# First attention of a two-layer transformer kernel on one Trainium2 core: the root polynomial's middle step on GpSimd, twelve root tiles and four log tiles, and a wide PSUM ring

## The chip, the cores and the metric

One core of one Trainium2 chip runs the whole program. The metric is the device time of one execution in microseconds (us). TensorE (PE), VectorE (DVE), ScalarE (ACT), GpSimd (POOL) and SyncE (SP) run their own instruction streams and meet only in semaphores.

## The reference, cut to what matters

Two layers, each attention plus a feed-forward part, over 2048 positions of width 128. The change lies in the attention of layer 0, which has 16 heads of width 8:

```python
q, k = _l2norm(to_heads(q)), _l2norm(to_heads(k))
cos = einsum('bhsd,bhtd->bhst', q, k)
g_dist = arccos(clip(cos, -1 + EPS, 1 - EPS))
attn_score = (1 + g_dist) ** -3.2
n_r, n_c = attn_score.sum(-1), attn_score.sum(-2)
k_tilde = n_r[..., :, None] ** -1 * attn_score * n_c[..., None, :] ** -1
probs = k_tilde / maximum(k_tilde.sum(-1), 1e-12)
out = einsum('bhst,bhtd->bhsd', probs, v)
```

So each head needs a 2048 x 2048 map of arccos, then of the power -3.2 (as Exp of -3.2 times Ln of 1 + angle), column sums, and a product with the values. The rest of the program (the projections, the feed-forward parts, the second attention) is as it was.

## The kernel before, in words

`stage_attention0` works head by head. The map of a head is 16 tiles of 128 keys x 2048 queries in float32, `wt[:, k, :]`. TensorE makes the raw material in PSUM. `square(h, g)` gives half a tile (two matmuls of 512 columns, L639) of the squared sine into one of the two 1024-wide slots of `m_ps`; `ring(h, r)` gives a chunk of 512 columns (L656, L660) into one of the two 512-wide slots of `r_ps`. A matmul of the ring waits until the chunk two before it has been read (`ring_read`).

There are two ways to the angle. A **root tile** (`NQ` = 8 of them) takes a Sqrt on ScalarE out of `m_ps` (L560, two halves), and then a polynomial on VectorE in `root_tile`: four chunks of L444 (U: the root against a ring chunk), four of L450 (V: into the single buffer `two`, shown by the profile as `base`), two of L456 (1024 wide, V plus a constant times U, all in SBUF; its semaphore is `cubic`), four of L463 (F: the last factor against a ring chunk). A **log tile** (`NL` = 8) takes Ln (L568), Sigmoid (L603) and Arctan (L607) on ScalarE with four chunks of L474 on VectorE between the last two. Afterwards all tiles get Ln with a bias (`theta`, L578, by the groups in `GROUPS`) and Exp with the column sum (`score`, L587). VectorE's `values` (L484, L486) turns the column sums into weighted values, and TensorE's `weigh(h, p)` (L671, four column groups) adds a tile into `o_ps`.

Order in a head. ScalarE: table load, roots 0 to 7, table load, logs, table load, sigmoids and arctans in pairs, table load, then `theta` and `score` in turn. VectorE: `values` of the last two tiles of the head before, root tiles 0 to 2 (`RA` = 3; `finish` copies `o_ps` to `o_sb`, L492, ahead of tile 2), `finish_rows`, the eight log tiles, root tiles 3 to 7 with `values` of the first tiles among them, `stack` (four pieces of L433, the next head's operand `mst`), `values`. TensorE: two `weigh` of the head before, then squares with ring chunks strewn among them by the list `ring_to`, worked out beforehand from a pace of 0.954 us a root, 0.625 us a chunk and 2.35 us for L456, then the rest of the ring with `turn_factors` (transposes for the next head, L629) and three `weigh` inside it, six `weigh`, `start` of the next head (squares 0 and 1, ring chunks 0 and 1), and five `weigh`. GpSimd has only `monomials` (L287 to L308) once a head, and waits for `turn_factors` of that head. SyncE loads `qst` and `kst` of the next head once the ring of a head has been issued. On every engine heads 1 to 14 are a hardware loop (`Fori`; ScalarE has all 16 in it), heads 0 and 15 are written out.

Of the kernel before, what the change touches and what calls it, by code (L numbers as in the profile page):

```python
# [6 lines left out]
ALU = mybir.AluOpType  # L7
# [8 lines left out]
S = 2048  # L16
D = 128
NT = S // P
# [13 lines left out]
NL = 8  # L32
# [27 lines left out]
def stage_project0(nc, io, sb):  # L60
# [3 lines left out]
    with ExitStack() as ctx:  # L64
# [49 lines left out]
        with nc.Block() as block:  # L114
# [91 lines left out]
            @block.gpsimd  # L206
            def _(eng):
                fac = sb["fac"]
                for i, f in enumerate(F_ROWS):
                    eng.memset(fac[:, 0, :, 3 * NMON + i:3 * NMON + i + 1], GQK * GQK)  # L210
                    eng.memset(fac[:, 1, :, 3 * NMON + i:3 * NMON + i + 1], -f * GQK * GQK)
                eng.wait_ge(qkn_ready, 1)
                monomials(eng, sb, 0, mono, mono_ready)
# [69 lines left out]
def monomials(eng, sb, h, mono, mono_ready):  # L283

    qkn, xs, pr, fac = sb["qkn"], sb["mono_x"], sb["mono_p"], sb["fac"]
    steps = 3 * h
    eng.tensor_copy(xs[:, :, :, :].rearrange("p x n d -> p n x d"),  # L287
                    qkn[:, :, :].rearrange("p n (x d) -> p n x d", x=2)[:, :, :, bass.ds(h * HD0, HD0)])\
       .then_inc(mono, 1)
    eng.wait_ge(mono, steps + 1)  # L290
# [7 lines left out]
    eng.wait_ge(mono, steps + 2)  # L298
# [7 lines left out]
    eng.wait_ge(mono, steps + 3)  # L306
# [5 lines left out]
def stage_attention0(nc, io, sb):  # L312
# [7 lines left out]
    RA = 3  # L320
    GROUPS = (0, 4, NL, NL + 5, NT - 2, NT - 1, NT)
    PAIRS = tuple(range(0, NL, 2)) + (NL,)
    NM0 = 2 * NT
    NRING = 12 * NQ + 4 * NL
    NCU = 2 * NQ
    NSG = len(PAIRS) - 1

    def q_at(j):
        return 12 * j if j < RA else 12 * j + 4 * NL

    def s_at(j):
        return 12 * RA + 4 * j

# [6 lines left out]
    ROOT_US, CHUNK_US, CUBE_US, LOAD_US, LAG_US = 0.954, 0.625, 2.35, 1.3, 1.2  # L340

    def ring_time(r):

        q, z = (r, 0) if r < s_at(0) else (s_at(0), r - s_at(0)) if r < s_at(NL) else (r - 4 * NL, 4 * NL)
        return (q + z) * CHUNK_US + (q // 12 + (q % 12 >= 8)) * CUBE_US
# [4 lines left out]
    ring_to = [2 + sum(1 for r in range(2, NRING) if ring_time(r - 1) + LAG_US <= root_time(g)) for g in range(NM0)]  # L350
    with ExitStack() as ctx:
# [20 lines left out]
        st_ps = m_ps[:, :, :].rearrange("p a b -> p (a b)").bitcast(F16)  # L372

# [5 lines left out]
        cubic, sig_done = sem("cubic"), sem("sig_done")  # L379
# [5 lines left out]
        def cols(k, n=P):  # L385
            return slice(k * n, (k + 1) * n)

        with nc.Block() as block:
# [24 lines left out]
            def _(eng):  # L413
                with eng.Fori(1, H) as h:

                    eng.wait_ge(fac_turned, 4 * h)
                    eng.wait_ge(mono_ready, 1)
                    monomials(eng, sb, h, mono, mono_ready)

            @block.vector  # L420
            def _(eng):
# [5 lines left out]
                def stack(h, j):  # L427

                    eng.wait_ge(fac_turned, 4 * h + j + 1)
                    if j == 0 and not (isinstance(h, int) and h == 0):  # L430
                        eng.wait_ge(ring_ps, NRING * h)
                    half = mst[:, j % 2, cols(j // 2, S // 2)]
                    eng.tensor_scalar(half, st_ps[0:KM, cols(j, S // 2)], -1.0 if j % 2 else 1.0, None, ALU.mult)\  # L433
                       .then_inc(mst_ready, 1)

                def root_tile(h, j):

                    at = q_at(j)
                    for i in range(NCH):
                        if i % 2 == 0:  # L440
                            eng.wait_ge(m0_read, NM0 * h + 2 * j + i // 2 + 1)
                        eng.wait_ge(ring_ps, NRING * h + at + i + 1)
                        u = wt[:, j, cols(i, BANK)]
                        eng.scalar_tensor_tensor(out=u, in0=u, scalar=-B1 * S_MIN * G4, in1=r_ps[:, (at + i) % 2, :],  # L444
                                                 op0=ALU.max, op1=ALU.subtract).then_inc(ring_read, 1)
                    for i in range(NCH):

                        eng.wait_ge(ring_read, NRING * h + at + i + 1)
                        eng.wait_ge(ring_ps, NRING * h + at + NCH + i + 1)
                        eng.scalar_tensor_tensor(out=two[:, cols(i, BANK)], in0=wt[:, j, cols(i, BANK)],  # L450
                                                 scalar=-K1 * G4, in1=r_ps[:, (at + i) % 2, :],
                                                 op0=ALU.add, op1=ALU.mult).then_inc(ring_read, 1)
# [5 lines left out]
                    for i in range(NCH):  # L458
                        if i % 2 == 0:
                            eng.wait_ge(cubic, NCU * h + 2 * j + i // 2 + 1)  # L460
                        eng.wait_ge(ring_ps, NRING * h + at + 2 * NCH + i + 1)
                        u = wt[:, j, cols(i, BANK)]
                        eng.scalar_tensor_tensor(out=u, in0=u, scalar=K3 * G4 * G4 * G4, in1=r_ps[:, (at + i) % 2, :],  # L463
                                                 op0=ALU.add, op1=ALU.mult).then_inc(ring_read, 1)

                def log_tile(h, j):

                    if j in PAIRS:
                        eng.wait_ge(sig_done, NSG * h + j // 2 + 1)
                    for i in range(NCH):  # L470
# [1098 lines left out]
```

## Time and profile before

| what | value |
|---|---|
| median of 3 runs | 3972.32 us (3971.55 to 3972.55) |
| the profiled execution | 3976.55 us, its span 3974.8 us |
| PE, DVE, ACT, POOL busy in the span | 3205.7, 2999.1, 3186.7, 1201.9 us |
| mean granted TensorE clock | 0.784 |
| last Exp of one head to the last Exp of the next | 133.1 us |
| part of the span that is the first attention's heads | about 118 to 2250 us |

The span is cut into busy time of each engine, and each idle stretch is put down to what released it. Times in a timeline count from the span's start. Instructions of one engine overlap a little in the records: the distance between starts is what an instruction takes of its engine, and it is below the recorded duration.

### The profile page before, as it was taken

To read this page: it belongs to the slowest core of one execution; us is meant where nothing else is said; L and a number is where in the kernel's file an instruction comes from. 1 tells how busy PE (TensorE), PEld (TensorE's weight loads), DVE (VectorE), ACT (ScalarE), POOL (GpSimd) and SP (SyncE) were. 2 spreads that over 40 slices of the span, in tenths; PEclk is the share of its full clock that TensorE was granted. 3 is DMA by queue.
4 is the path that set the end of the run, shared out by engine and by line. 5 is a ranking of instruction groups with operands and counts; after the bars stand their busy time and mean duration, and the time that the engine had idled before them with its cause. 6 is when DMAs were issued, how large, how long until landed. Compare 5 with 4: busy or idle time off the path is not lost. (4 is left out here: it accounts for less than half of the span.)

```text
span 3974.8 us, 59836 instructions
## 1 busy us (share of the span) xinstructions
PE 3205.7 (81%) x18880; PEld 1330.2 (33%) x18880; DVE 2999.1 (75%) x4716; ACT 3186.7 (80%) x2690; POOL 1201.9 (30%) x746
## 2 busy tenths in 40 slices
PE   4777787878787878787877675888888888888899
PEld 2311121112111211121111132355555555555547
DVE  6777877887788777877788798888787787788411
ACT  2799989998999899989999665488788787888822
POOL 2201100110011001101100043377677777777700
PEclk8776566556655665666567698799999999999999
DMA  1000000000000000000000126011001100110000
GB/s 39 31 7 7 0 6 6 6 0 6 6 6 0 6 6 6 0 6 6 6 0 10 35 89 188 22 30 36 23 22 38 28 23 23 39 28 22 20 17 11
DMA packets 59566, 85.93 MB, mean 22 GB/s; under 512 B 9808, under 2 KB 45904, under 8 KB 58960
## 3 DMA queue, kind: packets, MB, share of 16 engines
q1 hardware_dynamic: 59344, 83.06, 7.2%
q8 instruction: 128, 2.10, 0.2%
q14 instruction: 94, 0.77, 0.1%
HBM read 52.44 MB, written 30.54 MB: 21 GB/s over the span
## 5 line engine op out<-in xcount | busy, mean ns | idle before, releaser
L1086 POOL TENSOR_TENSOR lo<-pr,hi 128x1024 f16<-128x1024 f32 x384 | 915.6, 2409 | 391.3 <-ACT hi L1212 389.2
L1135 DVE TENSOR_REDUCE mx<-mx_ps 128x1 f32<-128x512 f32 x1024 | 660.3, 684 | 170.1 <-PE mx_ps L1250 166.4
L656 PE MATMUL r_ps<-qst,kst 72*128 72x512 bf16 x1024 | 576.1, 569 | 239.3 <-DVE wt L474 143.1
L1227 ACT ACTIVATE pr<-s_ps 128x1024 f32<-128x1024 f32 x512 | 531.3, 1038 | 269.0 <-PE s_ps L1271 238.9
L660 PE MATMUL r_ps<-mst 110*128 110x512 f16 (+1 forms) x1024 | 537.0, 535 | 158.7 <-DVE wt L444 115.9
L1212 ACT ACTIVATE hi<-pr 128x1024 f16<-128x1024 f32 x512 | 546.9, 1069 | 0.0
L287 POOL COPY mono_x<-two 128x256 f32 (+1 forms) x16 | 8.5, 531 | 1716.8 <-PE m_ps L629 1663.1
L1250 PE MATMUL mx_ps<-ka,qa 128*128 128x512 f16 x1024 | 385.5, 398 | 138.2 <-DVE mx L1135 115.4
L587 ACT ACTIVATE wt<-wt 128x2048 f32<-128x2048 f32 x256 | 484.9, 1895 | 0.5
L578 ACT ACTIVATE wt<-wt,theta_bias 128x8192 f32<-128x8192 f32 (+2 forms) x96 | 462.6, 4834 | 0.2
L1290 PE MATMUL pv_ps<-vh,hi 128*128 128x129 f16 x4096 | 432.3, 222 | 11.0 <-ACT sums L1218 5.8
L1269 PE MATMUL s_ps<-qa,ka 128*128 128x512 f16 x1024 | 396.8, 388 | 44.6 <-issue 22.4
L1290 PE MATMUL pv_ps<-vh,lo 128*128 128x65 f16 x4096 | 418.0, 194 | 0.0
L444 DVE SCALAR_TENSOR_TENSOR wt<-wt,r_ps 128x512 f32<-128x512 f32 x512 | 328.8, 684 | 116.9 <-PE r_ps L660 90.3
L474 DVE SCALAR_TENSOR_TENSOR wt<-wt,r_ps 128x512 f32<-128x512 f32 x512 | 329.5, 685 | 94.6 <-ACT wt L603 69.6
L1271 PE MATMUL s_ps<-qb,kb 65*128 65x512 f16 x1024 | 397.6, 388 | 0.0
L1290 PEld LDWEIGHTS pv_ps<-vh,hi 128*128 128x128 f16 x4096 | 372.6, 98 | 61.6 <-POOL lo L1086 10.9
L1290 PEld LDWEIGHTS pv_ps<-vh,lo 128*128 128x128 f16 x4096 | 366.1, 98 | 56.1 <-issue 3.5
L639 PE MATMUL m_ps<-mst 109*128 109x512 f16 x1024 | 333.1, 412 | 44.4 <-ACT wt L568 29.0
L463 DVE SCALAR_TENSOR_TENSOR wt<-wt,r_ps 128x512 f32<-128x512 f32 x512 | 330.6, 683 | 37.0 <-PE r_ps L656 31.1
L656 PEld LDWEIGHTS r_ps<-qst,kst 72*128 72x128 bf16 x1024 | 106.2, 104 | 733.1 <-DVE wt L474 379.7
L450 DVE SCALAR_TENSOR_TENSOR base<-wt,r_ps 128x512 f32<-128x512 f32 x512 | 328.2, 685 | 24.4 <-PE r_ps L660 9.2
(179 smaller groups left out, 4380.9 us busy)
## 6 DMA issues: line engine op xcount, KB each, us to landing
qk<-stg SPq DMA_DIRECT2D x6, 2048.0 KB, 13.6
vh<-v SPq DMA_DIRECT2D x16, 520.0 KB, 3.7
qa<-qk SPq DMA_DIRECT2D x16, 512.0 KB, 3.9
ka<-qk SPq DMA_DIRECT2D x32, 256.0 KB, 4.7
v<-v_st SPq DMA_DIRECT2D x3, 2080.0 KB, 7.9
qst<-parts_dram SPq DMA_DIRECT2D x144, 32.0 KB
kst<-parts_dram SPq DMA_DIRECT2D x144, 32.0 KB
qk<-stg SPq DMA_DIRECT2D x4, 1024.0 KB, 8.0
```

The costliest lines, as they stand in the source:

```text
L578: eng.activation(wt[:, k:k + many, :], wt[:, k:k + many, :], ACT.Ln, bias=theta_bias[:, 0:1], scale=-2.0 if k >= NQ else -KA / (G4 * G4 * ...
L587: eng.activation(wt[:, k, :], wt[:, k, :], ACT.Exp, scale=GEXP, accum_out=n_c[:, k:k + 1])\
L656: mm = eng.matmul(r_ps[:, r % 2, :], kst[:, cols(k)], qst[:, cols(n_, BANK)], start=True, stop=True)
L660: mm = eng.matmul(r_ps[:, r % 2, :], mst[0:rows, 1, cols(k)], mst[0:rows, 0, cols(n_, BANK)], start=True, stop=True)
L1086: eng.tensor_tensor(lo[:, i % NHL, :, :], pr_slot(i), hi[:, i % NHL, :, :], ALU.subtract).then_inc(lo_done, 1)
L1135: eng.tensor_reduce(mx4[:, q // NCH, q % NCH:q % NCH + 1], mx_ps[:, q % 2, :], AX.X, ALU.max)\
L1212: eng.activation(hi[:, i % NHL, :, :], pr_slot(i), ACT.Copy).then_inc(hi_done, 1)
L1227: eng.activation(pr_slot(i), s_ps[:, i % 2, :, :], ACT.Exp, scale=SM).then_inc(exp_done, 1)
L1250: eng.matmul(mx_ps[:, q % 2, :], qa[:, par, j * P:(j + 1) * P], ka[:, par, c * BANK:(c + 1) * BANK], start=True, stop=True).then_inc(mx_do ...
L1269: eng.matmul(s_ps[:, i % 2, n_, :], ka[:, par, k * P:(k + 1) * P], qa[:, par, w], start=True, stop=False)
L1271: mm = eng.matmul(s_ps[:, i % 2, n_, :], kb[0:HD1 + 1, par, k * P:(k + 1) * P], qb[0:HD1 + 1, par, w], start=False, stop=True)
L1290: mm = eng.matmul(pv_ps[:, j // 2, j % 2 * OW:j % 2 * OW + cols], half[:, i % NHL, n_, j * P:(j + 1) * P], vh[:, par, k, 0:cols], start=(k ...
```

## The change

`NL` goes from 8 to 4, so `NQ` from 8 to 12: per head twelve root tiles and four log tiles. `RA` goes from 3 to 4.

The step L456 leaves VectorE. GpSimd's `shift_and_multiply(h, j)` does it as four instructions of 1024 columns in SBUF: two `tensor_scalar` adds in place on `two` (semaphore `shifted`), then two `tensor_tensor` products with U into `wt` (semaphore `cubic`). On VectorE `root_tile` is split into `raised` (U), `folded` (V) and `closed` (F), and the order is U(j), V(j), F(j-1). As `two` is one buffer, V(j) waits for `cubic` of tile j-1. `monomials` is split too: `products(h+2)` comes after GpSimd's tile 4 of head h, `factors(h+2)` after tile 11, one head earlier than before. GpSimd's program is written out for all 16 heads.

The ring has 44 chunks of 512 columns (R1 = 44: U and V of tiles 0 to 3, F of tiles 0 to 2) in two slots, issued among the squares, and then 58 chunks of 1024 columns in three slots: the two of `m_ps`, free once all 32 squares are read, and `r_ps` as one. A wide chunk is two matmuls and one VectorE instruction. The wide part starts with U and V of tile 4, then the four log tiles (two chunks each), F of tile 3, and U, V, F for the rest.

`stack` is two instructions of 2048 columns, `turn_factors` two batches of 16 transposes, put ahead of the last two ring chunks. `weigh` of the head before has one tile left (15), after square 3; four `weigh` stand every third chunk from tile 8 on, five stand after consecutive chunks at the end of the ring. The groups of `theta` are now 4, 5, 4, 1, 1 and 1 tiles. VectorE does `values` of every tile of a head within that head, the last of them as the last thing in its loop body. Sigmoid and Arctan go tile by tile.

```diff
@@ constants
-NL = 8
+NL = 4
@@ GpSimd
-                with eng.Fori(1, H) as h:
-
-                    eng.wait_ge(fac_turned, 4 * h)
-                    eng.wait_ge(mono_ready, 1)
-                    monomials(eng, sb, h, mono, mono_ready)
+                def shift_and_multiply(h, j):
+
+                    at = v_at(j)
+                    half = 2 * BANK // width(at)
+                    for i in range(2):
+                        eng.wait_ge(ring_read, NRING * h + at + half * (i + 1))
+                        v = two[:, cols(i, 2 * BANK)]
+                        eng.tensor_scalar(v, v, -K2 * G4 * G4, None, ALU.add).then_inc(shifted, 1)
+                    for i in range(2):
+                        eng.wait_ge(shifted, NCU * h + 2 * j + i + 1)
+                        u = wt[:, j, cols(i, 2 * BANK)]
+                        eng.tensor_tensor(u, two[:, cols(i, 2 * BANK)], u, ALU.mult).then_inc(cubic, 1)
+
+                products(eng, sb, 1, mono)
+                eng.wait_ge(fac_turned, 2)
+                factors(eng, sb, 1, mono, mono_ready)
+                for h in range(H):
+                    for j in range(RA + 1):
+                        shift_and_multiply(h, j)
+                    if h + 2 < H:
+                        eng.wait_ge(mono_ready, h + 2)
+                        products(eng, sb, h + 2, mono)
+                    for j in range(RA + 1, NQ):
+                        shift_and_multiply(h, j)
+                    if h + 2 < H:
+                        eng.wait_ge(fac_turned, 2 * h + 4)
+                        factors(eng, sb, h + 2, mono, mono_ready)
@@ VectorE: the step that leaves
-                    for i in range(2):
-                        eng.wait_ge(ring_read, NRING * h + at + NCH + 2 * i + 2)
-                        u = wt[:, j, cols(i, 2 * BANK)]
-                        eng.scalar_tensor_tensor(out=u, in0=two[:, cols(i, 2 * BANK)], scalar=-K2 * G4 * G4, in1=u,
-                                                 op0=ALU.add, op1=ALU.mult).then_inc(cubic, 1)
@@ VectorE: V waits for GpSimd
+                def folded(h, j):
+
+                    at = v_at(j)
+                    w = width(at)
+                    for i in range(S // w):
+                        eng.wait_ge(ring_read, NRING * h + u_at(j) + i + 1)
+                        if j > 0 and i * w % (2 * BANK) == 0:
+                            eng.wait_ge(cubic, NCU * h + 2 * (j - 1) + i * w // (2 * BANK) + 1)
+                        eng.wait_ge(ring_ps, NRING * h + at + i + 1)
+                        eng.scalar_tensor_tensor(out=two[:, cols(i, w)], in0=wt[:, j, cols(i, w)],
+                                                 scalar=-K1 * G4, in1=slot(at + i),
+                                                 op0=ALU.add, op1=ALU.mult).then_inc(ring_read, 1)
@@ VectorE: a head
+                    for j in range(RA):
+                        raised(h, j)
+                        folded(h, j)
+                        if j > 0:
+                            closed(h, j - 1)
+                        if j == 2 and not first:
+                            finish(h - 1)
+                    if not first:
+                        finish_rows(h - 1)
+                    raised(h, RA)
+                    folded(h, RA)
+                    for j in range(NL):
+                        log_tile(h, j)
+                    closed(h, RA - 1)
+                    for j in range(RA + 1, NQ):
+                        raised(h, j)
+                        folded(h, j)
+                        closed(h, j - 1)
+                        if j == RA + 3:
+                            values(h, 0, GROUPS[1])
+                        if j == NQ - 2:
+                            values(h, GROUPS[1], GROUPS[2] - GROUPS[1])
+                    if not last:
+                        for x in range(2):
+                            stack(h + 1, x)
+                    values(h, GROUPS[2], GROUPS[3] - GROUPS[2])
+                    closed(h, NQ - 1)
+                    for p in range(GROUPS[3], NT):
+                        values(h, p, 1)
@@ TensorE: a head
+                        if g == 3 and not first:
+                            weigh(h - 1, NT - 1)
+                        for r in range(done, ring_to[g]):
+                            ring(h, r)
+                            if r == f_at(2) and not first:
+                                turn(h - 1)
+                        done = max(done, ring_to[g])
+                    for r in range(done, RE):
+                        ring(h, r)
+                        for p in range(NL):
+                            if r == u_at(RA + 4) + 1 + 3 * p:
+                                weigh(h, p)
+                        for p in range(NL, GROUPS[2]):
+                            if r == u_at(NQ - 1) + 1 + p - NL:
+                                weigh(h, p)
+                    if not last:
+                        for x in range(2):
+                            turn_factors(h + 1, x)
+                    ring(h, RE)
+                    ring(h, RE + 1, last)
```

## Rows read from the trace of the kernel before

**Rows 1.** Busy time by stage of one looped head (us; x instructions), last Exp to last Exp

```profile
core 0: us, PE busy (x) PEld busy (x) DVE busy (x) ACT busy (x) POOL busy (x), PEclk, DMA share, GB/s
776.57:799.88 23.31, 21.90 (x130) 6.38 (x122) 14.55 (x25) 16.41 (x18) 0.00 (x0) 1.00 0.04 9
...
850.71:909.69 58.98, 45.53 (x140) 10.94 (x144) 49.54 (x75) 58.93 (x39) 12.53 (x18) 0.51 0.03 7
sum 133.12, PE 106.11 PEld 26.35 DVE 106.97 ACT 122.87 POOL 12.53; mean PE 26.53 PEld 6.59 DVE 26.74 ACT 30.72 POOL 3.13
```

**Rows 2.** Timeline of ScalarE: start, us, operation, count, idle before

```profile
779.06 1.94 ACT L560 ACTIVATE wt<-m_ps 128x1024 f32<-128x1024 f32 x2 [1.21 <-PE m_ps L639]
786.61 13.25 ACT L560 ACTIVATE wt<-m_ps 128x1024 f32<-128x1024 f32 x14 [5.61 <-PE m_ps L639]
...
819.89 14.14 ACT L603 ACTIVATE wt<-wt 128x4096 f32<-128x4096 f32 x4
...
850.71 14.13 ACT L578 ACTIVATE wt<-wt,theta_bias 128x8192 f32<-128x8192 f32 x2
...
872.32 8.81 ACT L578 ACTIVATE wt<-wt,theta_bias 128x10240 f32<-128x10240 f32 x1
...
909.69 1.28 ACT L592 ACT_TABLE_LOAD   x1
```

**Rows 3.** Groups by line and form, 0 to 2400 us: busy, mean ns

```profile
L587 ACT ACTIVATE wt<-wt 128x2048 f32<-128x2048 f32 x256 | 484.9, 1895 | 0.5
...
L578 ACT ACTIVATE wt<-wt,theta_bias 128x2048 f32<-128x2048 f32 x48 | 95.4, 1987 | 0.0
```

**Rows 4.** Timeline of VectorE, heads 5 to 6 and the written-out head 15

```profile
774.82 0.17 DVE L486 TENSOR_TENSOR vh<-v,vh 128x8 f32<-128x8 f32 x1
778.59 0.16 DVE L484 RECIPROCAL vh<-n_c 128x1 f32<-128x1 f32 x1 [3.60 <-PE o_ps L671]
...
790.99 2.35 DVE L456 SCALAR_TENSOR_TENSOR wt<-base,wt 128x1024 f32<-128x1024 f32 x2
793.26 2.55 DVE L463 SCALAR_TENSOR_TENSOR wt<-wt,r_ps 128x512 f32<-128x512 f32 x4
795.73 2.51 DVE L444 SCALAR_TENSOR_TENSOR wt<-wt,r_ps 128x512 f32<-128x512 f32 x4
...
804.67 0.69 DVE L463 SCALAR_TENSOR_TENSOR wt<-wt,r_ps 128x512 f32<-128x512 f32 x1 [0.41 <-PE r_ps L656]
...
808.93 1.28 DVE L444 SCALAR_TENSOR_TENSOR wt<-wt,r_ps 128x512 f32<-128x512 f32 x2 [0.51 <-PE r_ps L660]
...
2106.30 0.16 DVE L484 RECIPROCAL vh<-n_c 128x1 f32<-128x1 f32 x1
```

**Rows 5.** Timeline of TensorE in the same head

```profile
803.17 1.04 PE L639 MATMUL m_ps<-mst 109*128 109x512 f16 x2
804.00 0.63 PE L656 MATMUL r_ps<-qst,kst 72*128 72x512 bf16 x1
...
851.76 3.62 PE L629 MATMUL m_ps<-ident_h,fac 128*111 128x128 f16 x32
...
904.09 7.52 PE L671 MATMUL o_ps<-wt,vh 128*32 128x512 f32 x48
```

**Rows 6.** GpSimd, the whole span by line and form: busy, mean ns

```profile
L957 POOL TENSOR_TENSOR hl<-ra,hl 128x512 f16<-128x512 f32 x64 | 74.0, 1156 | 454.3 <-ACT hl L913 454.3
...
L287 POOL COPY mono_x<-two 128x256 f32 x15 | 6.0, 398 | 1663.1 <-PE m_ps L629 1663.1
```

**Rows 7.** GpSimd by source line: ns min/median/max; one timeline row

```profile
L1086 POOL TENSOR_TENSOR lo<-pr,hi x384: 2118/2132/3120, 2536.2 to 3765.5; 128x1024 f16<-128x1024 f32 x192
...
L304 POOL CAST fac<-mono_p x32: 683/686/1677, 73.5 to 1927.3; 128x576 f16<-128x576 f32 x32
...
L305 POOL TENSOR_TENSOR mono_p<-mono_p x16: 927/1902/1954, 74.7 to 1928.0; 128x448 f32<-128x448 f32 x16
...
856.03 3.39 POOL L294 TENSOR_TENSOR mono_p<-mono_x 128x256 f32<-128x256 f32 x8
```

More of the change, by code:

```diff
@@ L212, in _ @@
                 eng.wait_ge(qkn_ready, 1)
-                monomials(eng, sb, 0, mono, mono_ready)
+                products(eng, sb, 0, mono)
+                factors(eng, sb, 0, mono, mono_ready)
             @block.scalar
@@ L296, in monomials, with factors @@
     last.then_inc(mono, 1)
-    eng.wait_ge(mono, steps + 2)
+def factors(eng, sb, h, mono, mono_ready):
+    pr, fac = sb["mono_p"], sb["fac"]
+    eng.wait_ge(mono, 3 * h + 2)
     cross = pr[:, 1, :, HD0:NMON]
@@ L386, in cols, with slot @@
             return slice(k * n, (k + 1) * n)
+        def slot(r):
+            if r < R1:
+                return r_ps[:, r % 2, :]
+            return m_ps[:, (r - R1) % 3, :] if (r - R1) % 3 < 2 else pair_ps
         with nc.Block() as block:
@@ L425, in _ @@
                 eng.tensor_copy(ident_h[:, :], ident[:, :]).then_inc(const_ready, 1)
[L427 to L433, printed above, removed]
-                       .then_inc(mst_ready, 1)
@@ L436, in root_tile, with stack, raised @@
[L436 to L441, printed above, removed]
+                def stack(h, x):
+                    eng.wait_ge(fac_turned, 2 * h + x + 1)
+                    eng.tensor_scalar(mst[:, x, :], st_ps[0:KM, cols(x, S)], -1.0 if x else 1.0, None, ALU.mult)\
+                       .then_inc(mst_ready, 1)
+                def raised(h, j):
+                    at = u_at(j)
+                    w = width(at)
+                    for i in range(S // w):
+                        if i * w % (2 * BANK) == 0:
+                            eng.wait_ge(m0_read, NM0 * h + 2 * j + i * w // (2 * BANK) + 1)
@@ L442, in root_tile @@
                         eng.wait_ge(ring_ps, NRING * h + at + i + 1)
-                        u = wt[:, j, cols(i, BANK)]
-                        eng.scalar_tensor_tensor(out=u, in0=u, scalar=-B1 * S_MIN * G4, in1=r_ps[:, (at + i) % 2, :],
+                        u = wt[:, j, cols(i, w)]
+                        eng.scalar_tensor_tensor(out=u, in0=u, scalar=-B1 * S_MIN * G4, in1=slot(at + i),
                                                  op0=ALU.max, op1=ALU.subtract).then_inc(ring_read, 1)
[L446 to L451, printed above, removed]
-                                                 op0=ALU.add, op1=ALU.mult).then_inc(ring_read, 1)
@@ new lines, in closed @@
+                def closed(h, j):
+                    at = f_at(j)
+                    w = width(at)
+                    for i in range(S // w):
+                        if i * w % (2 * BANK) == 0:
+                            eng.wait_ge(cubic, NCU * h + 2 * j + i * w // (2 * BANK) + 1)
+                        eng.wait_ge(ring_ps, NRING * h + at + i + 1)
+                        u = wt[:, j, cols(i, w)]
+                        eng.scalar_tensor_tensor(out=u, in0=u, scalar=K3 * G4 * G4 * G4, in1=slot(at + i),
@@ L608, in _ @@
[L608 to L618 removed]
+                    for j in range(NL):
+                        u = wt[:, NQ + j, :]
+                        eng.wait_ge(m0_read, NM0 * h + 2 * (NQ + j) + 2)
+                        eng.activation(u, u, ACT.Sigmoid, scale=-0.5).then_inc(sig_done, 1)
@@ new lines, in _ @@
+                    for j in range(NL):
+                        u = wt[:, NQ + j, :]
+                        eng.wait_ge(ring_read, NRING * h + s_at(j) + 2)
+                        eng.activation(u, u, ACT.Arctan, scale=1.0 / (GQK * GQK)).then_inc(atan_done, 1)
+                    eng.preload_act_table_set("natural_log_exp_and_others")
+                    theta(h, 0)
+                    for p in range(NT):
+                        if p + 1 in GROUPS[1:4]:
+                            theta(h, GROUPS.index(p + 1))
+                        if p == NT - 3:
+                            theta(h, NG - 2)
+                        if p == NT - 1:
+                            theta(h, NG - 1)
+                        score(h, p)
@@ L688, in head @@
                 def head(h, first=False, last=False):
-                    if not first:
-                        weigh(h - 1, NT - 2)
-                        weigh(h - 1, NT - 1)
                     done = 2
@@ L714, in head @@
                         start(h + 1)
-                    for p in range(NL + 1, NT - 2):
+                    for p in range(GROUPS[3] - 1, NT - 1):
                         weigh(h, p)
@@ L720, in _ @@
                 eng.wait_ge(const_ready, 1)
-                for j in range(4):
-                    turn_factors(0, j)
+                for x in range(2):
+                    turn_factors(0, x)
                 start(0)
@@ L727, in _ @@
                 head(H - 1, last=True)
-                weigh(H - 1, NT - 2)
                 weigh(H - 1, NT - 1)
```

193 lines of the change are left out of this document (88 added, 105 removed).

## The prediction

> **What bounds the kernel now.** The busy times of one looped head come first: 133.12 us from last Exp to last Exp, of which ScalarE works 122.87, VectorE 106.97, TensorE 106.11 and GpSimd 12.53 [rows 1]. ScalarE is the bound. Its timeline shows where its idle 10.25 us lie: 1.21 and 5.61 us at the start of a head, behind TensorE's last `weigh` instructions [rows 2], the rest in scraps of at most 1.3 us. So a head shrinks if ScalarE gets less work and nobody else becomes late. VectorE and TensorE have 26 us of room each, GpSimd 120.
>
> **ScalarE, alone.** Four tiles turn from log to root. A Sqrt half costs what a Ln half does (13.25/14 = 0.95), so only the Sigmoid and Arctan of four tiles go: eight tiles of Sigmoid take 14.14 [rows 2], Arctan the same, so half of both is 14.1 us. ScalarE's work falls to 108.8 us. That is the floor of a head, and 24.3 us under the present one.
>
> **VectorE, alone.** L456 goes: 16 instructions, 2.27 a pair start to start (790.99 to 793.26) [rows 4], 18 us. Four more root tiles bring 12 chunks each in place of 4: 32 chunks more at 0.62 (four in 793.26 to 795.73), 19.8 us. A 1024-wide instruction out of PSUM is not in the trace. Two narrow ones bound it above (1.24); the wide L456 with both inputs in SBUF gives 1.14. I take 1.15, as the fixed part is paid once; 58 of them save 5 us. VectorE ends near 104 us a head. A tile in the wide part is 6 x 1.15 = 6.9 us.
>
> **GpSimd, per tile.** Two products of 1024 columns: the row of L1086 has 2.13 us (median), L957 1.16 for 512 [rows 6, 7]; I take 2.07 start to start. Two adds of a constant in place: not in the trace. Below stand one-input instructions, 0.40 us for 256 columns and 0.69 for 576 [rows 6, 7], so 0.9 ns a column and 1.09 us for 1024; above stands the two-input product, 2.13. I take 1.05 start to start, since an add of a constant reads one stream as a cast does. With 0.3 of semaphores the cycle is 2 x 1.05 + 2 x 2.07 + 0.3 = 6.5 us against VectorE's 6.9: hidden, by 0.4 us. Twelve tiles and the monomials make 12 x 6.5 + 12.5 = 91 us of 133. `products` (3.4) falls under the eight log chunks, `factors` under the end of the head. L305 takes 1.90 us in most heads and 0.93 at its shortest [rows 7]: it meets L456, which reads SBUF twice. All wide steps of VectorE now read SBUF once, so that wait goes and none is priced.
>
> A rule of the Trainium skill speaks against the move: GPSIMD Engine Reference, section 3.1, gives about 1.8 cycles an element as the best of a tight loop (769 ns for 512 elements). By it an add of 1024 would be an estimated 1.54 us, the cycle 7.5, and GpSimd the slower one of the pair. The casts here, at 0.69 us for 576, are quicker than that rule; no run so far shows an add.
>
> **The new head, along its path** (0 is the last Exp of the head before). I follow what ends last.
>
> 1. VectorE's last `values` takes 0.5, then its loop jumps back. Before, the instruction after the jump starts 3.6 us after the one ahead of it (774.99 to 778.59), while in the written-out head 15 it follows at once (2106.30, no wait) [rows 4]. I read 3.6 us of jump. It lay under the last Exp; now it stands after it. U of tile 0 starts at 4.1.
> 2. The narrow part: 44 x 0.61 = 26.8, the copy of `o_ps` 0.6. TensorE issues square 3 and `weigh` 15 before ring chunk 3, about 1.8 us at full clock against 0.6 of cover: 1.2. V(1) waits for GpSimd's first products, as no F stands between: 1.8 for both halves (V(0)'s first half, then 1.05 + 1.05 + 2.07, against 0.6 + 0.6 + 2.4 on VectorE, and again for the second). The clock dips as it does before, and costs three waits of 0.4 to 0.6 [rows 4]: 1.5. VectorE reads chunk 43 at **36.0**. ScalarE alone would be done with 32 halves at 33, so its squares run at the ring's pace and it loses 5 to 6 us here.
> 3. The last squares wait behind the ring. ScalarE's last Ln half ends 2.8 later, and the first wide chunk needs all 32 read: 1.0 more. `finish_rows` fits in. **39.8.**
> 4. U, V of tile 4 and eight log chunks, 12 x 1.15 = 13.8: **53.6.** Sigmoids (1.77 a tile) are ahead of it. Last Arctan 1.9, table load 1.3 (row 909.69), `theta` of four tiles 7.07, three scores 5.7 (L587, 1.895 each [rows 3]), `theta` of five 8.7, a score 1.9: **80.2** [rows 2, 3].
> 5. VectorE comes to `values` of tiles 0 to 3 at 53.6 + 2.3 + 3 x 6.9 = 76.6 and waits 3.6. Then F(7) and F(8) take 2 x 6.9 from 80.7: 94.5. `theta` 2 holds tiles 5 to 8 and needs them; ScalarE has done its scores at 87.8, and idles 6.7 us. It ends at 101.6, score 8 at **103.5.**
> 6. `values` of 4 to 8, U, V of 11 and F(10): 104.0 + 6.9 = 110.9; ScalarE's own chain (scores 9 to 11, `theta` 3, score 12) is at 113.1, then `theta` 4, two scores, `theta` 5 and the last score: 2.0 + 3.8 + 2.0 + 1.9, **122.8** with all of TensorE's work hidden.
> 7. TensorE's drag. At half clock a wide chunk costs it 0.83 [rows 5], a `weigh` 1.25 (six in 7.52, row 904.09), the transposes 3.62. Four `weigh` at every third chunk ask 3 x 0.83 + 1.25 = 3.75 against 3.45 of VectorE: up to 1.0. Five at consecutive chunks ask 2.1 each against 1.15: F(10) ends at 113.5 instead of 110.9, 0.4 after ScalarE wants it. Behind them stand a last `weigh`, the transposes, the last ring chunks, `stack` and `values`, some 7.8 in all before F(11) ends at 121.3, where `theta` 5 wants it at 119.3: 2.0. Together 3.4 at half clock, near nothing at full. The granted clock is 0.51 here [rows 1], the level of 1.2 GHz, with TensorE waiting after each pair of chunks; the new ring gives it more work and fewer waits, and which level it then gets no row says. I take 2.2, two thirds.
>
> Head: **125.0**, 8.1 less than 133.1. Fifteen such intervals are 121.5. The first head gains about 6, and after the last Exp one `weigh` is left in place of seven, about 6. Sum 133.5: 3976.55 - 133.5 = 3843. The profiled execution is 4.2 above the median of the runs, so 3839.
>
> Hidden and free: SyncE's 18 loads for the next head begin some 4 us before the last Exp and are needed at ring chunk 16, near 15; table loads stay four; the smaller `stack` count saves under 0.3; TensorE's and GpSimd's longer streams have no jump on the path.
>
> **Rivals.**
>
> A, GpSimd's add costs the middle of its bounds, 1.6. The cycle is 7.6, 0.7 above VectorE's tile. It is paid at V(1) (1.1), over F(7), F(8) (1.4) and F(10), F(11) (1.0): 128.5 a head, 3976.55 - 4.6 x 15 - 10 - 4.2 = 3893. Taking 1.25 for a wide VectorE step in place of 1.15 gives about as much. The skill's loop rule, named above, would land here. For: no row shows an add on GpSimd. Against: the cast rows, which also read one stream and write one.
>
> B, **slower**: GpSimd sets the pace. If the add costs like a product (2.1), the cycle is 8.6: narrow part +5, F(7) and F(8) +3.4, F(10) and F(11) +3.4, tile 5 and 6 in part +0.5: 137.3 a head; with the first head 4 longer and the tail 6 shorter 3976.55 + 4.2 x 15 - 2 - 4.2 = 4033. It decides from a cycle of about 8.0, an add of 1.8: there the waits at V(j), with F(j-1) and U(j+1) queued behind each, have eaten the 8.1. The skill's section 4.1 of the same page says to leave such work to VectorE.
>
> C, also slower: TensorE stays at half clock in the narrow part. Then 42 chunks and 60 square matmuls at 0.42 [rows 5] are 43 us against the 32 of step 2, 11 to 12 more: 137 a head, 4029. Against: clock 1.00 at a head's start [rows 1].
>
> D, better: squares and GpSimd mesh without steps 2's waits, full clock throughout: 119 a head, 3976.55 - 14.1 x 15 - 12 - 4.2 = 3749.
>
> E, nothing is left of it: the waits of ScalarE in steps 2 and 5 (6 and 6.7) grow by 8 in all and eat the rest of the 14.1. It would take A and a full drag of TensorE together.
>
> **Chances.** Forecast (121 to 127.7) 0.62, A (to 132.5) 0.18, D 0.05, E (within 0.2%) 0.03, B 0.09, C 0.03. About 0.2%, 8 us, is what a measurement can tell from no change; that is half a microsecond a head. Faster 0.85, same 0.03, slower 0.12. The range runs from 3770 (120.4 a head) to 3925 (130.8).
>
> **What would show it.** Right: 24 Sqrt halves with idle of 5 to 6 us among them; U(0) 4 us after the last Exp; V(1) waiting for POOL and later V not; `values` waiting 3 to 4 us for Exp 3; ScalarE idle 6 to 7 before `theta` 2; GpSimd adds near 1.1 and products near 2.1. Wrong: V waits for POOL at every tile (B), clock 0.5 with VectorE waiting for `r_ps` early in a head (C), or no VectorE wait at the jump, which would give back 2 us.

## The result, and the profile after

The changed kernel takes 4219.24 us (median of 4, 4212.88 to 4225.39) against 3972.44 for the kernel before: a ratio of 1.062, 95% interval 1.0603 to 1.0637. It was forecast at 3839 and faster. It is 247 us slower, and even rival B's 4033 was too low.

One head of the profiled execution, from the table load after its last Exp to the next such load (busy time by stretch; columns as in [rows 1]):

```profile
core 0: us, PE busy (x) PEld busy (x) DVE busy (x) ACT busy (x) POOL busy (x), PEclk, DMA share, GB/s
1009.28:1155.45 146.17, 103.64 (x392) 23.44 (x388) 110.09 (x127) 110.44 (x83) 133.83 (x67) 0.74 0.02 4
```

ScalarE's work fell from 122.87 to 110.44 us, about as forecast (108.8). But GpSimd, at 12.53 before [rows 1], now works 133.83 of 146.17: it is the bound. (This head is one of the shorter; the mean from head to head is 147.9.) The profiled execution is 240.9 us longer than the one before: fifteen intervals of 14.9 make 223, the first head 23.5, and 5.7 come back after the last Exp. The groups of GpSimd, as in [rows 6], with the range of one instruction from the views by source line (L309 is the line that was L305 before):

```profile
L455 POOL TENSOR_SCALAR base<-base 128x1024 f32<-128x1024 f32 x384 | 1063.1, 2769 | 216.9 <-DVE base L510 189.4
L459 POOL TENSOR_TENSOR wt<-base,wt 128x1024 f32<-128x1024 f32 x384 | 907.8, 2385 | 15.4
L309 POOL TENSOR_TENSOR mono_p<-mono_p 128x448 f32<-128x448 f32 x16 | 14.9, 933 | 0.0
...
L455 POOL TENSOR_SCALAR base<-base x384: 2767/2768/2777, 128.5 to 2473.3; 128x1024 f32<-128x1024 f32 x192
L459 POOL TENSOR_TENSOR wt<-base,wt x384: 2337/2387/2427, 134.2 to 2478.5; 128x1024 f32<-128x1024 f32 x192
```

The add of a constant, taken at 1.05 us and bounded above by 2.13, takes 2.77, every one of 384. It is dearer than the product of two tensors. The timeline of GpSimd shows the cycle of one tile, 1086.95 to 1097.43, 10.5 us with no idle:

```profile
1086.95 5.62 POOL L455 TENSOR_SCALAR base<-base 128x1024 f32<-128x1024 f32 x2
1092.64 4.71 POOL L459 TENSOR_TENSOR wt<-base,wt 128x1024 f32<-128x1024 f32 x2
1097.43 5.62 POOL L455 TENSOR_SCALAR base<-base 128x1024 f32<-128x1024 f32 x2
```

and VectorE's timeline waits for it once or twice in each tile, at V (L510), with F and the next U queued behind:

```profile
1091.52 1.21 DVE L498 SCALAR_TENSOR_TENSOR wt<-wt,m_ps 128x1024 f32<-128x1024 f32 x1
1095.13 1.22 DVE L510 SCALAR_TENSOR_TENSOR base<-wt,m_ps 128x1024 f32<-128x1024 f32 x1 [2.40 <-POOL wt L459]
1097.47 1.22 DVE L510 SCALAR_TENSOR_TENSOR base<-wt,r_ps 128x1024 f32<-128x1024 f32 x1 [1.12 <-PE m_ps L730]
1098.61 2.34 DVE L523 SCALAR_TENSOR_TENSOR wt<-wt,m_ps 128x1024 f32<-128x1024 f32 x2
```

The profile puts the second wait, 1.12 us, down to TensorE's chunk that ends at 1097.45. But that V reads `r_ps`, which was written by 1092.69; what it needed was GpSimd's second product, which ends at 1097.35. In the tiles that follow, the same wait stands under GpSimd's name.

ScalarE pays at the end of that chain. The row that answers to the third `theta` of [rows 2], which had no wait, is now

```profile
1122.04 7.13 ACT L643 ACTIVATE wt<-wt,theta_bias 128x8192 f32<-128x8192 f32 x1 [16.95 <-DVE wt L523]
```

17 us of idle, where 6.7 were forecast.

### The profile page after: what moved, and what is told of

It reads as the page before. It is cut to its first block and busy times, and to the rows that moved or that the text cites. A ratio compares the mean times of both kernels' runs of the same rounds, so it can differ in the third digit from the quotient of the medians.

```text
span 4215.7 us, 60333 instructions
## 1 busy us (share of the span) xinstructions
PE 3277.6 (78%) x19392; PEld 1305.4 (31%) x19392; DVE 3038.8 (72%) x4012; ACT 2990.1 (71%) x2690; POOL 3145.7 (75%) x1514
## 5 line engine op out<-in xcount | busy, mean ns | idle before, releaser
L455 POOL TENSOR_SCALAR base<-base 128x1024 f32<-128x1024 f32 x384 | 1063.1, 2769 | 216.9 <-DVE base L510 189.4
L459 POOL TENSOR_TENSOR wt<-base,wt 128x1024 f32<-128x1024 f32 x384 | 907.8, 2385 | 15.4
L643 ACT ACTIVATE wt<-wt,theta_bias 128x8192 f32<-128x8192 f32 (+1 forms) x96 | 465.0, 4843 | 352.3 <-DVE wt L523 352.1
L734 PE MATMUL r_ps<-mst 111*128 111x512 f16 (+1 forms) x992 | 443.1, 500 | 255.1 <-DVE base L510 220.1
L510 DVE SCALAR_TENSOR_TENSOR base<-wt,r_ps 128x512 f32<-128x512 f32 (+1 forms) x384 | 319.6, 862 | 252.3 <-POOL wt L459 194.9
L624 ACT ACTIVATE wt<-m_ps 128x1024 f32<-128x1024 f32 x384 | 371.6, 1024 | 156.2 <-PE m_ps L704 153.9
L730 PE MATMUL m_ps<-qst,kst 72*128 72x512 bf16 x704 | 322.1, 555 | 177.2 <-DVE base L510 157.1
L704 PE MATMUL m_ps<-mst 109*128 109x512 f16 x1024 | 369.3, 452 | 25.2 <-ACT wt L624 14.5
L745 PE MATMUL o_ps<-wt,vh 128*32 128x512 f32 x2048 | 334.7, 751 | 63.1 <-DVE vh L545 63.1
L1365 PEld LDWEIGHTS pv_ps<-vh,lo 128*128 128x128 f16 x4096 | 365.8, 98 | 56.2 <-issue 3.2
L498 DVE SCALAR_TENSOR_TENSOR wt<-wt,r_ps 128x512 f32<-128x512 f32 (+1 forms) x368 | 300.1, 844 | 49.1 <-PE r_ps L734 30.8
```

The costliest lines, as they stand in the source:

```text
L455: eng.tensor_scalar(v, v, -K2 * G4 * G4, None, ALU.add).then_inc(shifted, 1)
L459: eng.tensor_tensor(u, two[:, cols(i, 2 * BANK)], u, ALU.mult).then_inc(cubic, 1)
L643: eng.activation(wt[:, k:k + many, :], wt[:, k:k + many, :], ACT.Ln, bias=theta_bias[:, 0:1], scale=-2.0 if k >= NQ else -KA / (G4 * G4 * ...
L734: mm = eng.matmul(slot(r)[:, cols(i, BANK)], mst[0:rows, 1, cols(k)], mst[0:rows, 0, rhs], start=True, stop=True)
L1365: mm = eng.matmul(pv_ps[:, j // 2, j % 2 * OW:j % 2 * OW + cols], half[:, i % NHL, n_, j * P:(j + 1) * P], vh[:, par, k, 0:cols], start=(k ...
```

## The experiments

Two theories stood after the result. **The instruction:** GpSimd's shift (the add of the constant) is 1.7 us dearer than forecast, and its cycle through the one buffer `two` sets the pace. **The shape:** twelve root tiles, the waits through one buffer and the wide ring cost the time by themselves. The first four runs tell them apart.

### The shift narrowed to 16 columns

```diff
-                        v = two[:, cols(i, 2 * BANK)]
+                        v = two[:, 2 * BANK * i:2 * BANK * i + 16]
```

> The changed kernel with GpSimd's shift narrowed from 1024 to 16 columns of each half, so most of the constant K2 is left out of the result and nothing else changes. Theory: GpSimd's cycle of 10.5 us a tile sets the pace, and without 5 us of it the path that the prediction followed returns: 122 to 126 us a head, about 3830 us in all. Rival: the twelve root tiles, the waits through one buffer or the wide ring cost the time by themselves; then it stays above 4050.

Measured: 3853.46 us, ratio 0.97 (0.967 to 0.973), a mean of 125.1 us from head to head. The prediction's path had 125.0. So 366 us of the change's time, more than its whole loss of 247, hang on 5 us a tile of GpSimd; the shape is sound. One head of it:

```profile
999.09:1122.85 123.76, 101.68 (x413) 23.83 (x413) 104.33 (x126) 109.77 (x82) 73.57 (x66) 0.77 0.02 5
```

### What the instruction costs by itself

Two probes put instructions on GpSimd in the first stage of the kernel before, where it is idle, each waiting for the one ahead of it. (Left out of both diffs: the buffers, the helper `link`, a first `memset` and, in the first, a last copy to float16.)

```diff
+                for w in (2 * BANK, BANK, P):
+                    link(eng.tensor_scalar(x[:, 0:w], x[:, 0:w], 0.5, None, ALU.add))
+                link(eng.tensor_scalar(y, x, 0.5, None, ALU.add))
+                link(eng.tensor_scalar(y, x, 0.5, None, ALU.mult))
+                link(eng.tensor_scalar(y, x, 0.5, 0.5, ALU.mult, ALU.add))
+                link(eng.tensor_scalar(probe_h[:, :], x, 0.5, None, ALU.add))
+                link(eng.tensor_tensor(z, x, y, ALU.add))
+                link(eng.tensor_tensor(z, x, z, ALU.mult))
+                link(eng.tensor_tensor(z, x, probe[:, 1, 0:1].to_broadcast([P, 2 * BANK]), ALU.add))
+                link(eng.tensor_copy(z, x))
```

> The kernel before, with twelve instructions of 1024 float32 columns on GpSimd in the idle start of the first stage, each waiting for the one before it; time unchanged. If the shift is dear by its kind, every tensor_scalar add of 1024 columns takes about 2.77 us here too, in place or not, and a copy about 1.1. If it is dear only for running in place or beside VectorE, the out-of-place one here takes about 1.1 to 1.6. The question for a remedy is tensor_tensor with a constant read with stride 0: about 2.1 if two streams set the price.

The timeline of GpSimd, in the order of the diff (the first row is the add in place at 1024, 512 and 128 columns):

```profile
3.90 4.96 POOL L225 TENSOR_SCALAR probe<-probe 128x1024 f32<-128x1024 f32 x3
8.95 2.77 POOL L226 TENSOR_SCALAR probe<-probe 128x1024 f32<-128x1024 f32 x1
11.80 2.80 POOL L227 TENSOR_SCALAR probe<-probe 128x1024 f32<-128x1024 f32 x1
14.69 1.04 POOL L228 TENSOR_SCALAR probe<-probe 128x1024 f32<-128x1024 f32 x1
15.81 2.88 POOL L229 TENSOR_SCALAR probe_h<-probe 128x1024 f16<-128x1024 f32 x1
18.77 2.34 POOL L230 TENSOR_TENSOR probe<-probe 128x1024 f32<-128x1024 f32 x1
21.19 2.34 POOL L231 TENSOR_TENSOR probe<-probe 128x1024 f32<-128x1024 f32 x1
23.61 1.89 POOL L232 TENSOR_TENSOR probe<-probe 128x1024 f32<-128x1024 f32 x1
25.57 1.04 POOL L233 COPY probe<-probe 128x1024 f32<-128x1024 f32 x1
```

The price comes neither from running in place nor from VectorE beside it: an add or a multiply alone costs 2.8 us out of place too, 2.88 into float16, and VectorE's first instruction starts at 7.37, when most of the adds in place are over. But the row of L228, with **two** operations (multiply, then add), takes 1.04, what a copy takes. I had not expected that. The second probe asks which forms are quick:

```diff
+                for w in (BANK, 2 * BANK):
+                    link(eng.tensor_scalar(x[:, 0:w], x[:, 0:w], 0.5, None, ALU.add))
+                for w in (BANK, 2 * BANK):
+                    link(eng.tensor_scalar(x[:, 0:w], x[:, 0:w], 1.0, 0.5, ALU.mult, ALU.add))
+                link(eng.tensor_scalar(y, x, 0.5, 0.5, ALU.add, ALU.mult))
+                link(eng.tensor_scalar(y, x, 0.5, 0.0, ALU.add, ALU.add))
+                link(eng.tensor_scalar(y, x, 0.5, 0.5, ALU.mult, ALU.mult))
+                link(eng.tensor_scalar(y, x, 0.5, 0.5, ALU.max, ALU.add))
+                link(eng.tensor_scalar(y, x, probe[:, 2, 0:1], None, ALU.add))
```

> As the first probe, with other forms of tensor_scalar on GpSimd. If a missing second operation is what costs, every form with two operations (multiply by 1 then add, add then multiply, add then add, multiply twice, max then add) takes 1.04 us for 1024 columns and 0.55 for 512, the one-operation add 2.77 and 1.4, and an add of a column (per-partition scalar) about 2.8. If only the pair multiply-add is quick, the other pairs take 2.8.

```profile
3.91 4.35 POOL L225 TENSOR_SCALAR probe<-probe 128x512 f32<-128x512 f32 x2
8.34 1.74 POOL L227 TENSOR_SCALAR probe<-probe 128x512 f32<-128x512 f32 x2
10.17 1.05 POOL L228 TENSOR_SCALAR probe<-probe 128x1024 f32<-128x1024 f32 x1
11.30 3.64 POOL L229 TENSOR_SCALAR probe<-probe 128x1024 f32<-128x1024 f32 x1
15.02 1.05 POOL L230 TENSOR_SCALAR probe<-probe 128x1024 f32<-128x1024 f32 x1
16.15 3.76 POOL L231 TENSOR_SCALAR probe<-probe 128x1024 f32<-128x1024 f32 x1
20.01 3.54 POOL L232 TENSOR_SCALAR probe<-probe 128x1024 f32<-128x1024 f32 x1
```

(x2 is 512 and then 1024 columns.) Neither guess held in full. Quick are multiply-add (L227), add-multiply (L228) and multiply-multiply (L230); the bare add (L225), add-add (L229), max-add (L231) and the add of a column (L232) are slow. Part of the times of L229, L231 and L232 may be waiting, as VectorE's normalization ran until 21.7 us there. But it is VectorE that waits most. Its 16 instructions take 4.20 us in the kernel before (13.53 to 17.73), and here, in the first and in the second probe:

```profile
13.64 14.41 DVE L162 TENSOR_SCALAR xn<-x_in,mv,tmp 128x128 f32<-128x128 f32 x16
...
13.85 7.87 DVE L162 TENSOR_SCALAR xn<-x_in,mv,tmp 128x128 f32<-128x128 f32 x16
```

The two products beside them in the first probe still took 2.34 each. The two kernels with probes took 3980.97 and 3979.25 us, one execution each, 6 to 7 us over the kernel before. Why a pair with a multiply is quick no run shows.

### The constant as a tensor

```diff
-                        eng.tensor_scalar(v, v, -K2 * G4 * G4, None, ALU.add).then_inc(shifted, 1)
+                        eng.tensor_tensor(v, v, shift_by[:, :].to_broadcast([P, 2 * BANK]), ALU.add).then_inc(shifted, 1)
```

> The changed kernel with the shift as tensor_tensor with a one-column constant read with stride 0. If tensor_tensor costs 2.1 to 2.4 whatever its second operand, the cycle falls from 10.5 to about 9.5, a head by 9 to 11 us, 4050 to 4090 us in all, still slower than before. If the stride-0 read costs as much as the tensor_scalar, no change at 4219.

Measured: 4062.09 us, ratio 1.0229 (1.0208 to 1.025). The read with stride 0 is a little cheaper than a full second tensor, and the cycle is 8.4 us:

```profile
L457 POOL TENSOR_TENSOR base<-base,shift_by 128x1024 f32<-128x1024 f32 x384 | 719.5, 1896 | 420.0 <-DVE base L514 419.8
...
1012.97 3.74 POOL L457 TENSOR_TENSOR base<-base,shift_by 128x1024 f32<-128x1024 f32 x2
1016.67 4.73 POOL L461 TENSOR_TENSOR wt<-base,wt 128x1024 f32<-128x1024 f32 x2
1021.37 3.73 POOL L457 TENSOR_TENSOR base<-base,shift_by 128x1024 f32<-128x1024 f32 x2
```

A head takes 137.6 us in the mean. Rival B had priced a cycle of 8.6 at 137.3, so its price for a head was near. What was expected before the run came out in its total, 4050 to 4090, by luck: the cycle fell by 2.1 us and not by 1.0, and each us of it was worth 4.9 a head, half of what was expected.

### Multiply by one

The obvious remedy, one line, the same values:

```diff
-                        eng.tensor_scalar(v, v, -K2 * G4 * G4, None, ALU.add).then_inc(shifted, 1)
+                        eng.tensor_scalar(v, v, 1.0, -K2 * G4 * G4, ALU.mult, ALU.add).then_inc(shifted, 1)
```

> The changed kernel with one instruction rewritten: the shift as multiply by 1.0, then add of the constant, the same values. If the form is what costs, the shift takes 1.04 us instead of 2.77, GpSimd's cycle is 2 x 1.12 + 2 x 2.42 = 7.1 us against VectorE's 6.8, a head takes 124.5 to 127.5 us, 3855 to 3905 us in all, and this is the fastest of all. If 2.77 us comes back in place beside VectorE, it stays at 4219.

Measured: 3881.95 us, ratio 0.977 (0.9757 to 0.9783), faster than both kernels. The group of the shift, and a cycle of 7.3 us (1070.91 to 1078.22) in GpSimd's timeline:

```profile
L455 POOL TENSOR_SCALAR base<-base 128x1024 f32<-128x1024 f32 x384 | 401.3, 1045 | 531.9 <-DVE base L510 521.2
...
1070.91 1.04 POOL L455 TENSOR_SCALAR base<-base 128x1024 f32<-128x1024 f32 x1
1072.25 1.05 POOL L455 TENSOR_SCALAR base<-base 128x1024 f32<-128x1024 f32 x1 [0.30 <-DVE base L510]
1073.38 4.76 POOL L459 TENSOR_TENSOR wt<-base,wt 128x1024 f32<-128x1024 f32 x2
1078.22 1.04 POOL L455 TENSOR_SCALAR base<-base 128x1024 f32<-128x1024 f32 x1
```

So 337 of the 366 us between the changed kernel and the narrowed shift come from the form of one instruction. GpSimd is not quite hidden: 7.3 us stand against VectorE's 6.8 in the wide part, and the second half of V waits in most tiles.

```profile
1070.94 1.22 DVE L510 SCALAR_TENSOR_TENSOR base<-wt,r_ps 128x1024 f32<-128x1024 f32 x1 [0.43 <-POOL wt L459]
```

### Half the step on each engine, and all of it on VectorE

```diff
+                    eng.wait_ge(ring_read, NRING * h + at + 2 * BANK // w)
+                    u = wt[:, j, 0:2 * BANK]
+                    eng.scalar_tensor_tensor(out=u, in0=two[:, 0:2 * BANK], scalar=-K2 * G4 * G4, in1=u,
+                                             op0=ALU.add, op1=ALU.mult).then_inc(cubed, 1)
```

in `folded`, with GpSimd left only the second half (its semaphores are left out here).

> The changed kernel with columns 0 to 1023 of the middle step back on VectorE as one instruction of L456's form, columns 1024 to 2047 on GpSimd as shift and product. If GpSimd's cycle is what costs, it is 5.3 us a tile now, VectorE has 8.0 a tile, and a head takes 126 to 130 us: 3880 to 3930 us in all, faster than both kernels. Rival: the two engines block each other, as VectorE's instruction reads SBUF twice while GpSimd reads it; each then waits up to 2.8 us a tile, 134 to 140 a head, 4000 to 4090.

Measured: 4003.45 us, ratio 1.0073 (1.0056 to 1.009), 134.5 us a head: the rival's band (134 to 140 a head). The blocking is there in GpSimd's shift, 0.91 us longer than its 2.77 (all 192 of them take 3.67 to 3.69), but it is not what costs:

```profile
L457 POOL TENSOR_SCALAR base<-base 128x1024 f32<-128x1024 f32 x192 | 705.9, 3676 | 812.0 <-DVE base L513 812.0
...
1136.45 3.68 POOL L457 TENSOR_SCALAR base<-base 128x1024 f32<-128x1024 f32 x1 [1.76 <-DVE base L513]
1140.22 2.40 POOL L460 TENSOR_TENSOR wt<-base,wt 128x1024 f32<-128x1024 f32 x1
...
1135.16 1.20 DVE L513 SCALAR_TENSOR_TENSOR base<-wt,r_ps 128x1024 f32<-128x1024 f32 x1
1136.29 1.21 DVE L518 SCALAR_TENSOR_TENSOR wt<-base,wt 128x1024 f32<-128x1024 f32 x1
```

VectorE's step (L518) starts first and reads SBUF twice. It ends at 1137.50, and the shift's end less its own 2.77 us is 1137.36: the record counts the shift from 1136.45, and it gets going when VectorE is done. The Trainium skill's SBUF — State Buffer, section Who interferes with whom, says that a VectorE instruction with two SBUF inputs contends with a GpSimd instruction that reads SBUF, and calls the shared ports an exclusive lock; the row agrees.

The rival's number came out, and not its mechanism. VectorE is not held: its tile takes 7.9 us (1128.37 to 1136.29), its six wide steps and the new one. GpSimd idles 1.76 us in each such tile, waiting for VectorE, so its 0.91 lies in slack. What lengthens the head is VectorE's own step on the path, which the forecast of 126 to 130 priced too low: the third `theta` starts 10.2 us later than with the narrowed shift (103.6 against 93.4), and ten steps of 1.13, 11.3 us, stand ahead of the F of tile 8 that it waits for.

```diff
+                    for i in range(2):
+                        eng.wait_ge(ring_read, NRING * h + at + 2 * BANK // w * (i + 1))
+                        u = wt[:, j, cols(i, 2 * BANK)]
+                        eng.scalar_tensor_tensor(out=u, in0=two[:, cols(i, 2 * BANK)], scalar=-K2 * G4 * G4, in1=u,
+                                                 op0=ALU.add, op1=ALU.mult).then_inc(cubic, 1)
```

> The changed kernel with the whole middle step back on VectorE as two instructions of L456's form after V; GpSimd keeps products and factors. VectorE has 6 x 1.13 + 2 x 1.13 = 9.1 us a tile and 131 us of work a head; with its waits for ScalarE 136 to 142 us a head, 4010 to 4110 us. It says what twelve root tiles are worth without GpSimd. If the ring or TensorE were the bound instead, it would be near the narrow-shift run, 3853.

Measured: 4193.8 us, ratio 1.0553 (1.0537 to 1.0569), 146.7 us a head, above what was expected. One stretch within a head:

```profile
997.30:1142.10 144.80, 107.80 (x388) 24.89 (x388) 129.33 (x149) 109.34 (x82) 9.38 (x16) 0.71 0.01 4
```

VectorE's work is the 131 forecast, near enough (129.33), but it is idle for 15.5 us where 5 to 11 were allowed, all of it for ScalarE. In this head 10.5 us of its waits are for TensorE's ring chunks and 4.3 for ScalarE. Over all heads, at U:

```profile
L491 DVE SCALAR_TENSOR_TENSOR wt<-wt,m_ps 128x1024 f32<-128x1024 f32 x144 | 173.3, 1212 | 42.1 <-PE m_ps L732 42.1
L491 DVE SCALAR_TENSOR_TENSOR wt<-wt,r_ps 128x512 f32<-128x512 f32 x256 | 166.8, 683 | 104.1 <-PE r_ps L732 55.3 <-ACT wt L622 46.9
```

So twelve root tiles are only worth having here with a cheap third engine; with the dear shift GpSimd was no better than VectorE alone (4219 against 4194).

### VectorE's loop written out

```diff
-                with eng.Fori(1, H - 1) as h:
+                for h in range(1, H - 1):
                     head(h)
```

> The kernel before with VectorE's heads 1 to 14 written out in place of the loop. The prediction read the 3.6 us ahead of the first values of a head as the loop's jump. If so, they are gone here, and the time is the same, as they lay under ScalarE's last Exp. If it is a wait on a semaphore, they stay.

Measured: 3970.76 us, one execution, against a median of 3973.41 before. In the kernel before, 3.60 us stood ahead of the first `values` after the jump [rows 4]; here it follows at once, and only the next one waits, for its Exp:

```profile
776.24 0.16 DVE L484 RECIPROCAL vh<-n_c 128x1 f32<-128x1 f32 x1
776.43 0.17 DVE L486 TENSOR_TENSOR vh<-v,vh 128x8 f32<-128x8 f32 x1
777.81 0.16 DVE L484 RECIPROCAL vh<-n_c 128x1 f32<-128x1 f32 x1 [1.21 <-ACT wt L587]
```

So the 3.6 us belong to the loop, as the prediction read them, and they cost nothing there.

### Two moves on top of multiply by one

With multiply by one, ScalarE idles 8.0 us before its third `theta` (1100.46 in that run's timeline), and VectorE 3.2 us before `values` of tiles 0 to 3. The first edit lets the third group end at tile 7:

```diff
-    GROUPS = (0, NL, NL + 5, NT - 3, NT - 2, NT - 1, NT)
+    GROUPS = (0, NL, NL + 5, NT - 4, NT - 2, NT - 1, NT)
```

> The two-operation kernel with the groups of theta at 4, 5, 3, 2, 1, 1 tiles instead of 4, 5, 4, 1, 1, 1. There ScalarE idles 8.0 us a head before its third group, waiting for F of tile 8. If that wait is on the path, a group that ends at tile 7 starts some 7 us earlier and a head loses 2 to 5 us: 3810 to 3850 us in all. If VectorE's own chain to F(11) sets the end of a head, nothing changes: 3882.

Measured: 3852.31 us, ratio 0.9697 (0.9683 to 0.9711), 124.7 us a head in place of 126.3. That is 1.6 a head, less than the 2 to 5 expected, and the time lies just above the 3810 to 3850 expected.

The second puts `values` of tiles 0 to 3, and the four `weigh` that need them, one tile later:

```diff
-                        if j == RA + 3:
+                        if j == RA + 4:
                             values(h, 0, GROUPS[1])
...
-                            if r == u_at(RA + 4) + 1 + 3 * p:
+                            if r == u_at(RA + 5) + 1 + 3 * p:
                                 weigh(h, p)
```

> As the split of the groups, with VectorE's values of tiles 0 to 3 one tile later (after F(7)) and TensorE's four weigh one tile later with them. VectorE's wait of 3.2 us for the fourth Exp goes; F(7) to F(11) end up to 3 us earlier. If VectorE's chain is the path, 1 to 3 us a head less than the split alone, 3770 to 3830 us; if ScalarE's is, the same as the split alone.

Measured: 3807.09 us (median of 6), ratio 0.9577 (0.9556 to 0.9599), 121.6 us a head. The third `theta` (three tiles now) starts without a wait; 2.0 and 2.8 us are left ahead of the two after it:

```profile
1058.17 5.40 ACT L643 ACTIVATE wt<-wt,theta_bias 128x6144 f32<-128x6144 f32 x1
1071.22 3.71 ACT L643 ACTIVATE wt<-wt,theta_bias 128x4096 f32<-128x4096 f32 x1 [1.97 <-DVE wt L523]
1081.51 2.00 ACT L643 ACTIVATE wt<-wt,theta_bias 128x2048 f32<-128x2048 f32 x1 [2.79 <-DVE wt L523]
```

Each edit took time off, so both ScalarE's and VectorE's chain were on the path. This is the best version, 170 us under the kernel before and 412 under the change.

## Why the prediction was wrong, step by step

**The step that failed** is "GpSimd, per tile": "above stands the two-input product, 2.13 ... I take 1.05 start to start, since an add of a constant reads one stream as a cast does". The add measured 2.77 us. The upper bound was no bound: how many inputs an instruction reads does not set its time here. A copy, a bare add and a multiply-add pair each read one, and take 1.04, 2.77 and 1.04; a product reads two, and takes 2.34. The second term was also short: the product, in float32 out, is 2.34 in the probe and 2.39 here, not the 2.13 of the rows with float16 out [rows 7], and it was taken at 2.07. Together, start to start, 2 x 2.85 + 2 x 2.4 = 10.5 us a tile in place of 6.5.

**The mechanism of rival B was right**, at a chance of 0.09, and its price of 4033 was short since it was worked out for a cycle of 8.6. Its decision point also held: 7.3 us leaves the change faster, 8.4 does not. Its price for each us of cycle did not: a head grows by 10 us for each between 7.3 and 8.4, and by 5 between 8.4 and 10.5. The same three stretches of a head, from ScalarE's timelines (us, counted from the table load after the last Exp, mean of 14 heads):

| run | GpSimd's cycle | start of first `theta` | start of third | next last Exp |
|---|---|---|---|---|
| forecast | 6.5 | 56.8 | 94.5 | 125.0 |
| shift of 16 columns | none | 54.4 | 93.4 | 125.1 |
| multiply by one | 7.3 | 56.2 | 95.4 | 126.3 |
| half on each engine | 6.1, in VectorE's 7.9 | 61.2 | 103.6 | 134.5 |
| constant as a tensor | 8.4 | 60.4 | 104.5 | 137.6 |
| the change | 10.5 | 66.4 | 114.5 | 147.9 |

The rows of the narrowed shift and of multiply by one bear out the rest of the working of a head, within 2.4 us at every mark; part of that is luck, as terms below were off in both directions. The rows of 8.4 and of 10.5 us lose in each stretch, as V(j) waits in each. Against the narrowed shift, the change loses 12 of its 23 us ahead of the first `theta`, and 9 over the tiles 5 to 8.

**Right:** ScalarE's floor (110.4 measured, 108.8 forecast); a wide VectorE step at 1.13 start to start (1.15 taken); the waits at V(1), 1.14 and 1.06 with multiply by one (1.8 taken for both halves); `values` waiting 3 to 4 us for the fourth Exp (3.2 with multiply by one); ScalarE idle before the third `theta` (8.0 against 6.7); the end of the wait on L305 (0.93 as L309 of the changed kernel, 1.90 in most heads before); TensorE's drag at the five `weigh` (waits of 0.7, 1.3, 0.3, 0.3 us for ring chunks there with multiply by one, 2.6 in all, as forecast).

**Wrong, and small:** the 3.6 us of jump did not come along. With multiply by one the last `values` ends at 1132.2 and U(0) starts at 1134.17, as soon as ScalarE's first root is there; in the change only 0.91 us lie between the two, and those are a wait for ScalarE too. It is a jump in the kernel before, as the written-out loop shows, but it is not a constant of loops. A hint at why: the instruction queue moved 94 packets before, 79 with VectorE's loop written out, 61 after the change. Whether a shorter body is kept and a longer one fetched again was not tried.

ScalarE's idle among the 24 roots was to be 5 to 6 us and is 3.5 with multiply by one. The three waits for a dip of the clock in the narrow part shrank to one of 0.41: there the granted clock of one head of that run was 1.00, and 0.70 from the first `theta` on. The short `values` products, which read SBUF twice, meet GpSimd at a head's end and wait up to 2.9 us, which was priced at nothing. And the first head was to gain 6 us: its last Exp comes 0.7 us later than before with the narrowed shift and 3.9 later with multiply by one. Why, no run separates.

## What to carry to other kernels

Before work moves to an engine, measure its very instruction there, in the form the code will have. A bound from a "similar" instruction did not hold here: with the same operands a copy took 1.04 us and an add of a constant 2.77. When a chain passes through one buffer, compare the two engines' cycles per tile; the path of a head was right to about 1% once the shift was cheap, and the answer was still on the wrong side for one term of 1.7 us, paid 24 times a head. And where a slow form is found, look for a longer one: adding a multiply by one made the instruction 2.6 times quicker.

## What the runs showed of the hardware

- GpSimd, 1024 float32 columns: `tensor_scalar` with a bare add or multiply 2.77 to 2.80 us (2.88 into float16), with a multiply-add pair, either order, or two multiplies 1.05, as a copy; with add-add or max-add slow (3.64 and 3.76, some of it perhaps waiting). The Trainium skill's GPSIMD Engine Reference, section 3.1, has about 1.8 cycles an element as a tight loop's best, an estimated 1.54 us here: the quick form beats it and the bare add is far above it.
- `tensor_tensor` on GpSimd takes 2.34 us for 1024 columns with float32 out, and 1.89 if one input is a single column read with stride 0.
- A GpSimd instruction that reads SBUF while VectorE runs one with two SBUF inputs is recorded as longer by what is left of VectorE's (3.68 in place of 2.77, in all 192). The other way round, VectorE's 16 instructions of 128 columns took 14.41 us beside GpSimd's probe in place of 4.20.
- The jump of one VectorE loop costs 3.6 us; that of the changed kernel's shorter body at most the 0.91 us between the last `values` and the first U.
